# Cross-attention over 224 head steps: the weighted sum lags one step, turned probabilities get two buffers, denominators go to GpSimd

## What is computed

```python
q = x1 @ Wq
kv = x2 @ Wkv
k, v = jnp.split(kv, 2, axis=-1)
q, k, v = map(_split_heads, (q, k, v))
attn = jnp.einsum('bhid,bhjd->bhij', q, k) * SCALE
attn = jax.nn.softmax(attn, axis=-1)
out = jnp.einsum('bhij,bhjd->bhid', attn, v)
...
return out @ Wo + bo
```

## Time and profile before

| what | value |
|---|---|
| median of 3 runs | 1561.71 us (1561.35 to 1567.66) |
| profiled execution: its time | 1565.5 us |
| profiled execution: its span | 1563.8 us |
| TensorE busy over the span | 1468.7 us (94%) |
| VectorE busy | 1242.0 us (79%) |
| ScalarE busy | 970.9 us (62%) |
| GpSimd busy | 604.6 us (39%) |
| mean granted clock of TensorE | 0.97 |

### The profile page before, as it was taken

One profiled execution on the slowest core, in us unless ns is written; L12 is line 12 of the kernel. 1 busy time (PEld: TensorE's weight loads), 2 busy tenths in 40 slices (PEclk: granted clock), 3 DMA queues, 4 the chain that ended last, 5 costly groups with the idle time before them and its releaser, 6 DMA issues. The chain is left out here.

```text
span 1563.8 us, 24194 instructions
## 1 busy us (share of the span) xinstructions
PE 1468.7 (94%) x8657; PEld 1303.5 (83%) x8657; DVE 1242.0 (79%) x2278; ACT 970.9 (62%) x1807; POOL 604.6 (39%) x519
## 2 busy tenths in 40 slices
PE   6999999999999999999999999999977989999479
PEld 5988998899889888988898889889865878888248
DVE  6888888888888888888888888888975356666764
ACT  4777777777777777777777777777651245555121
POOL 6334343434343434343434343433300256665330
PEclk9999999999999999999999999999997899999779
DMA  5000000000000000000000000000007122220600
GB/s 182 1 1 25 1 25 1 24 1 24 1 25 1 25 1 25 1 25 1 25 1 25 1 25 1 1 1 1 1 28 296 74 72 70 70 70 24 282 1 4
DMA packets 9099, 57.13 MB, mean 37 GB/s; under 512 B 2120, under 2 KB 2719, under 8 KB 7968
## 3 DMA queue, kind: packets, MB, share of 16 engines
q1 hardware_dynamic: 8992, 55.73, 9.6%
HBM read 55.60 MB, written 0.13 MB: 36 GB/s over the span
## 5 line engine op out<-in xcount | busy, mean ns | idle before, releaser
L314 POOL CAST V<-Vraw 128x512 fp32r<-128x512 f32 x189 | 115.8, 613 | 654.4 <-ACT Vraw L405 654.4
L369 ACT CAST K<-ps 64x448 fp32r<-64x448 f32 x448 | 236.4, 528 | 142.6 <-PE ps L532 133.1
L397 ACT ACTIVATE pT<-ps 128x896 fp32r<-128x896 f32 x224 | 206.3, 921 | 161.9 <-PE ps L558 161.7
L435 DVE TENSOR_TENSOR K<-ps,K 64x448 fp32r<-64x448 f32 x448 | 278.8, 622 | 13.3 <-ACT K L369 3.4
L493 DVE TENSOR_TENSOR pT<-ps,pT 128x896 fp32r<-128x896 f32 x224 | 244.6, 1092 | 31.9 <-ACT pT L397 8.3
L315 POOL TENSOR_TENSOR V<-Vraw,V 128x512 fp32r<-128x512 f32 x189 | 242.2, 1281 | 15.2
L443 DVE TENSOR_REDUCE nmx<-ps 128x1 f32<-128x896 f32 x224 | 242.2, 1081 | 0.0
L643 PEld LDWEIGHTS ps<-pT,V 128*128 128x128 f32 x1568 | 214.3, 189 | 17.0 <-DVE pT L493 7.5
L643 PE MATMUL ps<-pT,V 128*128 128x256 f32 x1568 | 222.5, 281 | 6.1 <-DVE pT L493 6.1
L379 ACT ACTIVATE prob<-ps,nm 128x896 f32<-128x896 f32 x224 | 224.3, 1001 | 0.0
L602 PE MATMUL ps<-ident,prob 128*128 128x128 f32 x1568 | 209.0, 274 | 0.0
(11 more groups left out here) (306 smaller groups left out, 2389.9 us busy)
## 6 DMA issues: line engine op xcount, KB each, us to landing
raw<-in_ctxT SPq DMA_DIRECT2D x14, 896.0 KB, 4.7
d_raw<-in_ctxT SPq DMA_DIRECT2D x14, 896.0 KB, 4.6
w<-in_w SPq DMA_DIRECT2D x2, 4096.0 KB, 16.8
wg<-in_wg SPq DMA_DIRECT2D x1, 4352.0 KB, 25.7
wu<-in_wu SPq DMA_DIRECT2D x1, 4352.0 KB, 16.8
wd<-in_wd SPq DMA_DIRECT2D x1, 4352.0 KB, 26.7
e_ea<-in_alog SPq DMA_DIRECT2D x1, 2048.0 KB, 7.3
wq<-in_wq SPq DMA_DIRECT2D x1, 1024.0 KB, 5.2
```

The source lines that it names most:

```text
L369: nc.scalar.copy(K[halves[s], slot, cols], ps[halves[s], piece_bank(p), 0:HK]).then_inc(sem("kh_ready"), 1)
L397: nc.scalar.activation(pT[:, :, 0, :], pT_ps, ACT.Copy).then_inc(sem("pTh_ready"), 1)
L435: ins = nc.vector.tensor_tensor(K[halves[1 - s], slot, cols], ps[halves[s], piece_bank(p), 0:HK], K[halves[s], slot, cols].bitcast(F32), A ...
```

## The change

The weighted sum of step u-1 is issued in step u, at the same place at the end of TensorE's step; in step u the turned partial sum is that of u-2. The turned probabilities `pT` get two buffers. On VectorE the order in an iteration becomes `low_parts(u+4)`, low half of the probabilities, `update_sums(u-2)`, `add_parts(u-1)`, `max_step(u+2)`. `al` and `rs` are kept for a whole chunk (two buffers by chunk), and GpSimd folds 16 denominators at a time into `den`, one chunk later; only for the last chunk VectorE still does it step by step. To make room for the second `pT`, the tiles `wg0`, `bg`, `b2`, `wx`, `bx`, `wxp`, `wdt`, `bdt`, `dskip`, `wr1`, `br1` are allocated after the call of `stage_context` (that block of the diff, a pure move of the three `norm_` functions and the call, is left out here).

```diff
-        pT = sb("pT", [P, NT, 2, P], F32R, keep)
+        pT = [sb(f"pT{i}", [P, NT, 2, P], F32R, keep) for i in range(2)]
...
-        al = sb("al", [P, 4], F32, keep)
-        rs = sb("rs", [P, 4], F32, keep)
+        al = sb("al", [P, 2, H0], F32, keep)
+        rs = sb("rs", [P, 2, H0], F32, keep)
...
+                def update_den(c):
+                    pool.wait_ge(sem("exp_done"), H0 * (c + 1))
+                    link(pool, nc.gpsimd.tensor_tensor(den[:, :], den[:, :], al[:, c % 2, :], ALU.mult), "pool_chain")
+                    nc.gpsimd.tensor_tensor(den[:, :], den[:, :], rs[:, c % 2, :], ALU.add).then_inc(sem("den_done"), 1)
+
                 for u in range(steps - HG):
                     if u % HG < NT:
                         split_values(v_steps.index(u))
+                    if u % H0 == 1 and u > 1:
+                        pool.wait_ge(sem("den_done"), u // H0 - 1)
+                        update_den(u // H0 - 1)
...
                     act.wait_ge(sem("max_done"), u + 1)
-                    if u >= 4:
-                        act.wait_ge(sem("u_added"), u - 3)
+                    if h == 0 and u >= 2 * H0:
+                        act.wait_ge(sem("den_done"), u // H0 - 1)
...
                 def update_sums(u):
-                    h, b = u % H0, u % 4
-                    dve.wait_ge(sem("p_turned"), u + 2)
-                    nc.vector.scalar_tensor_tensor(U[:, h, :], U[:, h, :], al[:, b:b + 1], O_ps,
+                    par, h = (u // H0) % 2, u % H0
+                    dve.wait_ge(sem("p_turned"), u + 3)
+                    nc.vector.scalar_tensor_tensor(U[:, h, :], U[:, h, :], al[:, par, h:h + 1], O_ps,
                                                    ALU.mult, ALU.add).then_inc(sem("u_added"), 1)
...
                 for u in range(steps):
-                    h, b = u % H0, u % 4
+                    par, h = (u // H0) % 2, u % H0
+                    if 1 <= u and u - 1 + AHEAD < steps:
+                        low_parts(u - 1 + AHEAD)
+                    dve.wait_ge(sem("pTh_ready"), u + 1)
+                    nc.vector.tensor_tensor(pT[u % 2][:, :, 1, :], pT_ps, pT[u % 2][:, :, 0, :].bitcast(F32),
+                                            ALU.subtract).then_inc(sem("pTl_ready"), 1)
+                    if u >= 2:
+                        update_sums(u - 2)
                     if u >= 1:
                         add_parts(u - 1)
-                        if u - 1 + AHEAD < steps:
-                            low_parts(u - 1 + AHEAD)
-                    dve.wait_ge(sem("pTh_ready"), u + 1)
-                    nc.vector.tensor_tensor(pT[:, :, 1, :], pT_ps, pT[:, :, 0, :].bitcast(F32),
-                                            ALU.subtract).then_inc(sem("pTl_ready"), 1)
-                    if u >= 1:
-                        update_sums(u - 1)
-                    if u >= H0:
-                        dve.wait_ge(sem("u_added"), u - H0 + 1)
-                    nc.vector.tensor_scalar(den[:, h:h + 1], den[:, h:h + 1], al[:, b:b + 1],
-                                            rs[:, b:b + 1], ALU.mult, ALU.add)
                     if u + 2 < steps:
                         max_step(u + 2)
-                    m = (u - (steps - H0)) // 2 - 1
-                    if u > steps - H0 and u % 2 == 0:
-                        scale_sums(m)
+                    if u >= steps - H0:
+                        dve.wait_ge(sem("den_done"), chunks - 1)
+                        nc.vector.tensor_scalar(den[:, h:h + 1], den[:, h:h + 1], al[:, par, h:h + 1],
+                                                rs[:, par, h:h + 1], ALU.mult, ALU.add)
+                    if u >= steps - H0 + 3 and u % 2 == 1:
+                        scale_sums((u - (steps - H0) - 3) // 2)
+                update_sums(steps - 2)
                 add_parts(steps - 1)
...
+                def weighted_sum(u):
+                    h, g = u % H0, u // HG
+                    pe.wait_ge(sem("pTl_ready"), u + 1)
+                    if u >= 1:
+                        pe.wait_ge(sem("o_added"), u)
...
+                    for k in range(NT):
+                        mm = nc.tensor.matmul(OT_ps, V[g % 2][:, k, h % HG, :],
+                                              pT[u % 2][:, k, :, :].rearrange("p a q -> p (a q)"),
+                                              start=(k == 0), stop=(k == NT - 1))
+                    mm.then_inc(sem("pv_done"), 1)
...
                     pe.wait_ge(sem("exp_done"), u + 1)
-                    if u >= 2:
-                        pe.wait_ge(sem("u_added"), u - 1)
+                    if u >= 1:
+                        pe.wait_ge(sem("pTl_ready"), u)
+                    if u >= 3:
+                        pe.wait_ge(sem("u_added"), u - 2)
...
-                    if u >= 1:
-                        mm = turn_sums(u - 1)
+                    if u >= 2:
+                        mm = turn_sums(u - 2)
                     mm.then_inc(sem("p_turned"), 1)
...
+                        if u >= 2:
+                            pe.wait_ge(sem("o_added"), u - 1)
...
                         piece(p)
+                    if u >= 1:
+                        if u in v_steps:
+                            pe.wait_ge(sem("vraw_ready"), v_steps.index(u) + 1)
+                        weighted_sum(u - 1)
...
+                pe.wait_ge(sem("u_added"), steps - 2)
+                turn_sums(steps - 2).then_inc(sem("p_turned"), 1)
+                weighted_sum(steps - 1)
+                turn_heads((4, 5, 6), 7)
+                pe.wait_ge(sem("u_added"), steps - 1)
                 turn_sums(steps - 1).then_inc(sem("p_turned"), 1)
```

More of the change, by code:

```diff
@@ L96, in build @@
         keep("zero", [P, 1])
[L97 to L107, removed]
         def norm_vector(dve, n):
@@ L136, in build @@
         stage_context(nc, t, sb, sem, link, ps, norms, v)
+        keep("wg0", [P, KT, E0])
+        keep("bg", [P, E0])
+        keep("b2", [E0, D])
+        keep("wx", [P, KT, D])
+        keep("bx", [P, KT])
+        keep("wxp", [P, KT, DTR + 2 * NST])
+        keep("wdt", [DTR, D])
+        keep("bdt", [1, D])
+        keep("dskip", [P, D])
+        keep("wr1", [P, KT, E1])
+        keep("br1", [P, E1])
         with ExitStack() as experts:
@@ L372, in exp_step @@
                 def exp_step(u):
-                    par, h, b = (u // H0) % 2, u % H0, u % 4
+                    par, h = (u // H0) % 2, u % H0
                     act.wait_ge(sem("max_done"), u + 1)
-                    if u >= 4:
-                        act.wait_ge(sem("u_added"), u - 3)
-                    nc.scalar.activation(al[:, b:b + 1], nm[:, 1 - par, h:h + 1], ACT.Exp,
+                    if h == 0 and u >= 2 * H0:
+                        act.wait_ge(sem("den_done"), u // H0 - 1)
+                    nc.scalar.activation(al[:, par, h:h + 1], nm[:, 1 - par, h:h + 1], ACT.Exp,
                                          bias=nm[:, par, h:h + 1], scale=-1.0)
                     nc.scalar.activation(prob[:, :, :], S[u % 2], ACT.Exp, bias=nm[:, par, h:h + 1],
-                                         scale=1.0, accum_out=rs[:, b:b + 1]).then_inc(sem("exp_done"), 1)
+                                         scale=1.0, accum_out=rs[:, par, h:h + 1]).then_inc(sem("exp_done"), 1)
                 for p in range(AHEAD):
@@ L396, in _ @@
                     act.wait_ge(sem("p_turned"), u + 1)
-                    nc.scalar.activation(pT[:, :, 0, :], pT_ps, ACT.Copy).then_inc(sem("pTh_ready"), 1)
+                    nc.scalar.activation(pT[u % 2][:, :, 0, :], pT_ps, ACT.Copy).then_inc(sem("pTh_ready"), 1)
                     if u + 1 < steps:
@@ L558, in turn_sums @@
                     return nc.tensor.transpose(O_ps, osb[:, :], ident[:, :])
+                def weighted_sum(u):
[3 more added lines that the diff above has]
+                        pe.wait_ge(sem("o_added"), u)
+                    if h % HG == 0:
+                        if g == 0:
+                            pe.wait_ge(sem("first_vl"), NT)
+                        else:
+                            pe.wait_ge(sem("v_split"), NT * g)
+                    for k in range(NT):
[3 more added lines that the diff above has]
+                    mm.then_inc(sem("pv_done"), 1)
                 def turn_heads(pairs, bank):
@@ L633, in _ @@
                         project(range(0, 4))
[L634 to L646, removed]
                     if u == steps - 3:
@@ L649, in _ @@
                         turn_heads((0, 1, 2, 3), 7)
-                    if u == steps - 1:
-                        turn_heads((4, 5, 6), 7)
+                pe.wait_ge(sem("u_added"), steps - 2)
[3 more added lines that the diff above has]
+                pe.wait_ge(sem("u_added"), steps - 1)
                 turn_sums(steps - 1).then_inc(sem("p_turned"), 1)
```

## The result

The changed kernel takes 1639.7 us (median of 4 runs, 1639.25 to 1642.14), the kernel before 1562.7 on the same chip: a ratio of 1.0489, 95% interval 1.0472 to 1.0506. It is slower by 77 us; the forecast was 1628, with a range of 1602 to 1668. The profiled execution took 1642.1 us with a span of 1640.3. Medians are over executions at the usual clock: one execution of the kernel before (1836.1 us, mean granted clock 0.74) and one of the eighth run's kernel (2083.2 us, 0.65) are left out.

What follows compares the result with a forecast made beforehand. TensorE's queue was taken to set the pace, with a VectorE ring outgrowing its 5.14 us step; +67.6 + 1.9 + 2.3 - 0.9 - 4 = +66.9 us on the median 1561.7 gave 1628 us, range 1602 to 1668.

Steps and rivals of the forecast that it cites:

- The ring: Steady head steps: piece, weighted sum, `add_parts`, `max_step`, `low_parts`, next piece take 5.37 us instead of 5.06, +67.6 us.
- short end: VectorE, `add_parts` to the maximum: 0.34 us possible instead of 0.46, which makes the step 5.25 us.
- long end: VectorE, line 446 to what follows it: at most 0.21 us instead of 0.13.
- The denominators: Moved to GpSimd: no gain, two operations of 1.1 us per update covered by its waits; last chunk 10 x 0.19 = +1.9 us.
- `scale_sums`: Last chunk, four in the ring at 0.58 us each: +2.3 us, or +6.3 at 1.57 each beside GpSimd.
- Head and tail: First step without a weighted sum -0.9 us; tail after step 218 -4 us, bounds -8 and 0.
- mark: Start of `add_parts` on VectorE, 0.03 us after the weighted sum's last matmul, used to clock each step.
- The clock: Sign for the forecast: TensorE's granted clock stays 1.00 despite waits of 1.7 us in steps without values.
- no change: Rival B, the whole kernel: time stays the same, which would need a ring of 5.06 us; chance 0.03.
- faster: Rival A: ring stays hidden, waits ahead of pieces and turns go, tail brings 4; about 1529 us; chance 0.04.
- Slower by the clock: Rival C: TensorE's idle pieces lower its clock in steps without values, +95 us, about 1723; chance 0.05.
- GpSimd's operations been uncovered: Rival D: GpSimd's denominator operations not hidden by its waits, +14 us on top, 1642; chance 0.03.

Runs made afterwards that it cites:

- eighth run: Maximum ahead of the wait, denominators updated earlier, and weighted sum ahead of the piece in steps without values: 1555.3 us, 0.9935 of the kernel before.
- fifth run: Changed kernel with GpSimd's denominator update issued at the first step of each chunk, ahead of `split_values`: 1635.7 us, 1.0442 of the kernel before.
- the kernel with the order alone: Kernel before with only the maximum moved behind the wait in `add_parts`, ahead of `low_parts`: 1634.1 us, 1.0439 of the kernel before.
- sixth run: Changed kernel with both `max_step` ahead of `add_parts` and the denominators updated one block earlier: 1554.9 us, 0.9934 of the kernel before.
- first run: Changed kernel with `max_step` swapped back ahead of `add_parts`, the rest kept: 1562.5 us, 0.9983 of the kernel before.
- third run: Changed kernel with one more VectorE instruction in steps 0 to 207, between `max_step` and `low_parts`: 1762.8 us.
- additional instruction beside: Changed kernel with one more VectorE instruction in steps 0 to 207, ahead of the wait in `add_parts`: 1636.6 us.

## Why the forecast was right, and where its sizes were off

**The ring.** The mechanism was the one named: `max_step` queued behind the wait in `add_parts`, `low_parts` behind it, the next piece behind that. The steady length was forecast as 5.37 and is 5.39 (1115.2 / 207). Two of its links were off in opposite ways, and that they cancel to within 0.02 is luck: `add_parts` to the maximum is 0.34 (504.30 to 504.64), the short end that I had named, not 0.46; from line 453 to `low_parts` it is 0.24 (505.76 to 506.00), beyond my long end of 0.21, not 0.13. The piece to the sum is 2.38 (507.31 to 509.69) where I took 2.36 behind a stall. Over steps 2 to 208 the ring's excess over my number is 1115.2 - 207 x 5.37 = 3.6 us.

**The denominators.** The wait of the earlier trace rows did cover GpSimd's two operations in the first twelve updates (GpSimd still waits 2.9 us for the next block behind them), and each takes 0.22 us, not 0.55. The step that failed is the one next to it: I looked at ScalarE's new wait for `den_done` and not at VectorE's, which is in the diff, and so put the last chunk at 0.19 us per step only. It cost 6.0 us (step 209 took 11.55 us where the ring with its denominator is 5.55): 4.5 of waiting, and the rest in TensorE's slower matmuls behind it. The fifth run took it away (5.54). The 0.19 was right: steps 211 to 217 alternate between 5.55 and 6.15, the longer ones with a `scale_sums`.

**`scale_sums`.** 0.60 us each in the ring, as against 0.58; none overlapped with GpSimd.

**Head and tail.** The first step saved the 0.9 us (the start of the head steps came 1.4 later, the mark of step 1 0.5 later). The tail gained 6.4 us by the observed mark of step 218 and 7.4 by the one that I had reckoned from (1148.95), where I had 4. Not all of that is the lag's: the kernel with the order alone needs 25.9 us for the same stretch (1217.59 to 1243.46), against 30.9 before and 24.5 after. And part of the 30.9 is the clock: before, TensorE was granted 0.60 from 1169 to 1172 us and 0.71 from 1170 to 1181, while with the order alone and in the sixth run it had 1.00 through the whole tail. How the gain divides between the clock, the order and the lag was not tested. The last step before the tail lasted 7.48 us (1224.67 to 1232.15) instead of 6.15, with TensorE at its lower clock from 1229 us to its end (0.50, after 2.50 us of idle time ahead of the piece), which nothing in my sum had.

**The clock.** It stayed at 1.00 through the steady part, in spite of 1.74 us of idle time in each eighth step. Windows of the changed kernel (columns as in rows 1):

```profile
200.00:1000.00 800.00, 774.19 (x4491) 667.44 (x4491) 626.94 (x1040) 546.33 (x1022) 306.42 (x298) 1.00 0.04 12
1175.00:1178.30 3.30, 3.30 (x14) 3.04 (x15) 1.05 (x2) 0.90 (x2) 0.00 (x0) 0.57 0.00 0
```

**The sum.** +67.6 for the ring was +71.2; the wait for `den_done` +6.0 and the slow step 218 +1.3 were missing; the tail was 3.4 better by my own mark. 66.9 + 3.6 + 6.0 + 1.3 - 3.4 + 0.7 for the stages behind + 1.4 for the later start is 76.5, the difference of the spans. The last two are no part of the change's cost that any run shows: both vary as much between the other kernels. The rivals: "no change" and "faster" needed the maximum to stay off the ring, and the first run shows what they would have given, 1562. "Slower by the clock" would have shown below 1.00 in the window above; it was near all the same: 2.31 us of idle time in place of 1.74 were enough for it in 8 of 26 steps of the third run, at 1.5 us each and not 3.5. And had GpSimd's operations been uncovered, GpSimd would not have stood waiting behind them, as it did for 2.9 us.

## What to carry to other kernels

When an instruction that waits is moved in an engine's queue, list what now stands behind it and follow each of these until it comes back to the wait: the length of that ring, not the engine's busy share, is the time of a step. A lag between two engines' stages only pays if the work that the wait used to let through still gets ahead of it; here swapping two statements was worth 77 us, and the lag, with the order that goes with it, some 7 us behind step 208. And look at every new wait once at the edge of the loop, where a producer's schedule ("one step into the next chunk") may lie behind the consumer's.

## What the runs showed of the hardware that I had not expected

- `low_parts` never started before the end of its predecessor on VectorE (0.01 to 0.04 us after it in both kernels), while the maximum and line 453's followers start about 0.08 us before it. A spacing read between two instructions is not that of another pair: 0.13 and 0.24 us behind the same line 453. The cause was not tested.
- Behind 4.75 us of idle time TensorE's granted clock was 0.57 for 3.3 us, and behind 2.50 us in step 218 it was 0.50; behind 1.74 us in every eighth step it stayed 1.00. With 2.31 us in every eighth step (third run) it fell in 8 of 26 cases, and each cost 1.5 us.
- The stretch from a stalled piece to the next mark is not quite a constant: 2.38 us in the changed kernel, 2.35 with the order alone, 2.34 and 2.32 with the additional instruction beside and in the ring. Its cause was not tested.
